# Ternary feed-forward of a perceiver kernel: both products of a tile in a row, its second activation first, the integers on POOL

## The reference

```python
def _layernorm(x, axis=-1, eps=1e-05):
    ...
def activation_quant(x, num_bits=8):
    ...
    s = qp / jnp.clip(jnp.max(jnp.abs(xf), axis=-1, keepdims=True), EPS, None)
    return (jnp.clip(jnp.round(xf * s), qn, qp) / s).astype(x.dtype)
def bit_linear(x, w):       # quantised x (8 bits) by ternary w
    ...
def rms_norm(x, weight, eps=RMS_EPS):
    ...
    return weight * (xf * jax.lax.rsqrt(var + eps)).astype(x.dtype)
h = jax.nn.silu(bit_linear(x, w_gate)) * bit_linear(x, w_up)   # 1024 rows x 1024
h = rms_norm(h, ln_weight)
return bit_linear(h, w_down)                                   # 1024 rows x 256
```

## Time and profile before

| what | us |
|---|---|
| median of 3 runs | 792.42 (791.86 to 793.72) |
| the profiled execution, its own time | 794.29 |
| its span, from the first to the last instruction | 792.1 |
| PE busy | 692.1 (87%) |
| DVE busy | 587.2 (74%) |
| ACT busy | 426.1 (54%) |
| POOL busy | 371.4 (47%) |
| the ternary layer in the span | from 208.82 (its first transposes) to 274.95 (end of its last `add`) |
| mean granted clock of TensorE, as a share of full speed | 0.943 |

### The profile page before, as it was taken

How to read it: one execution, slowest core, us unless ns; L and a number is a source line. 1 busy time by engine, 2 the same in 40 slices (tenths; PEclk the granted TensorE clock), 3 DMA queues, 4 the chain that set the end, 5 groups by cost and what they waited for, 6 DMA issues and landing times. The chain is left out here.

```text
span 792.1 us, 15843 instructions
## 1 busy us (share of the span) xinstructions
PE 692.1 (87%) x5487; PEld 466.5 (59%) x5490; DVE 587.2 (74%) x1156; ACT 426.1 (54%) x1314; POOL 371.4 (47%) x317
## 2 busy tenths in 40 slices
PE   5997899997666599999996899889999999999776
PEld 4664677786324354434334676567777776776644
DVE  4466799766788566656674889888888898788487
ACT  2565777653467312222335787156555645559664
POOL 1503555382246124334494555366676766666100
PEclk9999999999679579999996999999999999999989
DMA  6455000000300030720010000012211313320001
GB/s 197 122 172 226 1 2 1 2 1 1 93 2 1 0 113 19 235 69 26 1 40 1 2 2 1 21 42 61 61 52 48 110 62 97 83 90 3 1 3 52
DMA packets 33571, 41.91 MB, mean 53 GB/s; under 512 B 15072, under 2 KB 23264, under 8 KB 32608
## 3 DMA queue, kind: packets, MB, share of 16 engines
q1 hardware_dynamic: 33504, 41.06, 16.9%
HBM read 40.00 MB, written 1.05 MB: 52 GB/s over the span
## 5 line engine op out<-in xcount | busy, mean ns | idle before, releaser
L2094 POOL TENSOR_TENSOR ra_direct<-ra_direct,ra_crossed 128x512 f32<-128x512 f32 x64 | 81.2, 1268 | 80.2 <-DVE ra_crossed L2270 80.0
L717 ACT ACTIVATE c_probs<-bank,c_neg_max 128x128 f32<-128x128 f32 x256 | 91.2, 382 | 29.2 <-DVE c_neg_max L800 29.2
L2270 DVE SCALAR_TENSOR_TENSOR ra_crossed<-bank,ra_bias,ra_sin 64x512 f32<-64x512 f32 x128 | 95.9, 750 | 1.9
L753 POOL TENSOR_TENSOR c_probs<-c_probs,c_inverse 128x512 f32<-128x512 f32 x64 | 66.5, 1040 | 62.1 <-DVE c_inverse L771 62.1
L1557 POOL TENSOR_TENSOR r_turned<-r_times_a,r_times_b 128x1024 f32<-128x1024 f32 x24 | 56.4, 2351 | 72.3 <-DVE r_times_b L1756 72.3
L717 ACT ACTIVATION_READ_ACCUMULATOR c_probs<-bank,c_neg_max 128x1 f32 x256 | 56.6, 221 | 0.0
L2222 ACT ACTIVATE ra_probs_t<-bank 64x256 f32<-64x256 f32 x64 | 24.1, 377 | 58.4 <-PE bank L2164 58.0
L2228 ACT ACTIVATE ra_probs<-ra_masked,ra_neg_max 128x64 f32<-128x64 f32 x128 | 43.0, 337 | 18.2 <-DVE ra_neg_max L2290 17.9
L1837 POOL TENSOR_TENSOR ra_w_lo<-ra_raw,ra_w_hi 128x768 f16<-128x768 f32 x32 | 52.6, 1645 | 0.0
L58 PE MATMUL bank<-xt_hi,ra_w_hi 128*128 128x512 f16 x128 | 49.1, 383 | 0.9 <-PEq L599 0.9
L58 PE MATMUL bank<-xt_hi,ra_w_lo 128*128 128x512 f16 x128 | 49.0, 383 | 0.0
(11 more groups left out here) (280 smaller groups left out, 2093.7 us busy)
## 6 DMA issues: line engine op xcount, KB each, us to landing
ra_raw<-l_attn_w_dram SPq DMA_DIRECT2D x32, 384.0 KB, 3.0
wq<-l_wq_dram SPq DMA_DIRECT2D x16, 256.0 KB, 2.8
wo<-l_wo_dram SPq DMA_DIRECT2D x16, 256.0 KB, 3.4
wkcq<-l_wkcq_dram SPq DMA_DIRECT2D x16, 192.0 KB, 2.8
ra_wo<-l_attn_wo_dram SPq DMA_DIRECT2D x1, 2048.0 KB, 10.1
wqr<-l_wqr_dram SPq DMA_DIRECT2D x16, 96.0 KB, 2.9
wkv<-l_wkv_dram SPq DMA_DIRECT2D x16, 64.0 KB, 3.0
x_res<-x_dram SPq DMA_DIRECT2D x2, 512.0 KB, 7.5
```

Of the source, the lines that this page charges most:

```text
L717: e = nc.scalar.activation(probs[u][:, n, :], score_bank[u][q][:, n - q * HP, :], ACT.Exp, bias=neg_max[u][:, n:n + 1], accum_out=total[u] ...
L753: nc.gpsimd.tensor_tensor(out=probs[u][:, at, :], in0=probs[u][:, at, :], in1=inverse[u][:, at].unsqueeze(2).broadcast_to([P, HP, L]), op= ...
L2094: nc.gpsimd.tensor_tensor(out=direct[e][k][:], in0=direct[e][k][:], in1=crossed[k][:], op=ALU.add).then_inc(roped, 1)
L2270: ins = nc.vector.scalar_tensor_tensor(dst[out_lo:out_lo + rows].rearrange("p t (b s) -> p (t b) s", b=2), src[lo:lo + rows], bias[e][lo:l ...
```

## The change

The second `multiply` of a tile moves up on DVE, right behind the first. The second `silu` of a tile moves to the head of ACT's step. `integers` leaves DVE and goes to POOL, between the power of tile i-1 and the weighting of tile i. PE's list is the same.

```diff
--- before.py
+++ after.py
@@ -1298,14 +1298,30 @@
             nc.gpsimd.memset(magic[:], ROUND).then_inc(filled, 1)
             inputs.rstd(pool, PAIRS_X - 1)
             first.gpsimd(pool)
-            for t in range(TILES):
+            def integers(t):
+                pool.wait_ge(rounded, t + 1)
+                wait(pool, h_turned, t - 1)
+                nc.gpsimd.tensor_scalar(h_int[t % 2][:], hw[t % 2][:], ROUND, QUANT_MAX,
+                                        ALU.subtract, ALU.min).then_inc(h_ready, 1)
+
+            def weigh(t):
                 pool.wait_ge(multiplied, 2 * t + 2)
                 wait(pool, h_ready, t - 1)
                 nc.gpsimd.tensor_tensor(out=hw[t % 2][:], in0=h[t % 2][:], in1=m.ln_weight[:],
                                         op=ALU.mult).then_inc(weighted, 1)
+
+            def size(t):
                 pool.wait_ge(mean_done, t + 1)
                 nc.gpsimd.tensor_tensor(out=rms[:, t:t + 1], in0=mean_sq[:, t:t + 1], in1=m.minus_half[:],
                                         op=ALU.pow).then_inc(rms_done, 1)
+
+            for i in range(STEPS - 1):
+                if has(i - 1):
+                    size(i - 1)
+                if has(i - 2):
+                    integers(i - 2)
+                if has(i):
+                    weigh(i)
             for q in range(2):
                 ln.rstd(pool, q)
 
@@ -1395,12 +1411,12 @@
             keep_x(1)
             silu(0, 0)
             for i in range(STEPS):
+                if has(i):
+                    silu(i, 1)
                 if has(i - 1):
                     sum_squares(i - 1)
                 if has(i - 2):
                     round_h(i - 2)
-                if has(i):
-                    silu(i, 1)
                 if i in TURNS:
                     keep_x(TURNS[i])
                 if has(i + 1):
@@ -1443,12 +1459,6 @@
                 nc.vector.tensor_scalar(down_scale[:, at], h_max[:, at], m.ffn_mean[:, 2:3], 1.0 / QUANT_MAX,
                                         ALU.mult, ALU.mult)
 
-            def integers(t):
-                dve.wait_ge(rounded, t + 1)
-                wait(dve, h_turned, t - 1)
-                nc.vector.tensor_scalar(h_int[t % 2][:], hw[t % 2][:], ROUND, QUANT_MAX,
-                                        ALU.subtract, ALU.min).then_inc(h_ready, 1)
-
             def add(t):
                 dve.wait_ge(down_done, t + 1)
                 nc.vector.scalar_tensor_tensor(m.x[:, t, :], down_bank[t % 2], down_scale[:, t:t + 1],
@@ -1458,13 +1468,9 @@
             for i in range(STEPS):
                 if has(i):
                     multiply(i, 0)
+                    multiply(i, 1)
                 if has(i - 1):
                     sizes(i - 1)
-                if has(i - 2):
-                    integers(i - 2)
-                if has(i):
-                    multiply(i, 1)
-                if has(i - 1):
                     scales(i - 1)
                 if i == STEPS - 1:
                     ln.scale(dve, 0)
```

## The result

| kernel | median us | ratio to the kernel before | 95% interval |
|---|---|---|---|
| before | 792.14 (4 runs) | | |
| changed | 820.67 (4 runs, 819.05 to 821.31) | 1.0354 | 1.0332 to 1.0376 |

The change costs 28.5 us, where 6.9 were forecast. The profiled execution's span is 818.9 us, 26.8 more than before. The ternary layer, from its first transposes to the end of its last `add`, is 96.50 us long (207.74 to 304.24) where it was 66.13, so it lost 30.37 us.

The account below looks back on a forecast made before the run. DVE's own list was taken as the bound in steps with a fold, 5.47 us; afterwards a loop through the transposes. Terms +0.60, +5.73, -0.28 gave +6.05, clock +0.88: +6.9 us, 792.4 to 799.3, range 795.5 to 803.5.

Parts of the forecast that it names:

- Onto POOL: Integers moved to POOL: one instruction per tile was taken at 1.05 us, bounds 0.95 to 2.36 or 2.78 us.
- the integers are dear: Rival: POOL's integers take 2.36 us, giving 808.5 us, or 2.78, giving some 811; chance 10%.
- The loop: Third layer, transposes to next transposes through ACT, DVE and POOL: 6.81 us with a fold against 5.47, 5.95 without.
- to the first transposes: Piece 1, up to the layer's first transposes: second multiply ahead of mean square and power, +0.60 us.
- five loops: Piece 2, from the first transposes to tile 5's: 32.74 us against 27.01 before, +5.73.
- from tile 5's transposes to the end: Piece 3, to the last `add`: tile 6's integers +0.36, its `add` starting earlier -0.64, together -0.28 us.
- The power: POOL's power in each step: 0.55 us without DVE's integers beside it, where step 6 had 0.87.
- The clock: PE at its lower clock level after long waits: 0.88 us a loop, one of three loops counted, +0.88.
- What would show it: Profile signs: period 6.0 us without a fold, 6.8 with; near 8 means the integers' price was wrong.

Follow-up runs that it names:

- e1: Kernel of only one-input POOL instructions, nothing running beside them, against no kernel: subtract with min took 3.62 us, the pairs the program had used 1.04.
- e2: Changed kernel with POOL's integers made by add and multiply instead of subtract and min, limit at 127 left out: 798.54 us, 1.0075 of the kernel before.
- e9: Changed kernel with integers by add and multiply, that instruction run twice per tile, first into a spare tile: 807.35 us, 1.0220 of the kernel before.
- e3: Changed kernel with the integers back on DVE between sizes and scales, the rest of the change kept: 795.72 us, 1.0038 of the kernel before.
- e6: Kernel before with integers still on DVE but between first multiply and magnitude, and ACT rounding first: 788.88 us, 0.9963 of the kernel before.
- e10: Kernel before with only the integers moved to POOL, behind the power, made by add and multiply: 794.32 us, 1.0039 of the kernel before.
- e5: Kernel before with integers on POOL by add and multiply, ahead of the power, and ACT rounding first: 785.85 us, 0.9908 of the kernel before.

## Why the prediction was wrong

The time lies 17 us above the range, and one term did nearly all of it.

**The step that failed** is "Onto POOL": "1.05 us, which I take". The rows behind it were an interpolation over the number of columns, between rows whose pairs of operations were min with max and multiply with add. The slope of 0.82 ns a column was right and belongs to those pairs only. Subtract with min takes 3.63 us. The one row that warned, a single multiply of the same size at 2.78 us, was set aside because its rows have gaps; e1 shows 2.78 us without gaps. So the reason given was false, and 2.78 was no upper bound either. The rule of the Trainium skill (GPSIMD Engine Reference, Key points), a factor of about 2 against DVE, was nearer in direction but gave 1.37 us. Against DVE's 0.69 us for subtract with min in e1, POOL's dear pair is 5.2 times as long (3.62) and the cheap one 1.5 times (1.04; DVE wasn't timed with it).

**The rival "the integers are dear"** was the right one, at 10%. It was priced at seven places and at most 2.78 us. With 3.63 us and the 8.7 us per us between e2 and e9, neither of which uses the changed kernel's time, the forecast of 799.3 becomes 799.3 + 8.7 x 2.58 = 821.7, and 820.67 was measured.

**The loop** was right. The pieces of the layer, in us:

| piece | forecast | with 3.63 for 1.05 | measured in the change | measured in e2 |
|---|---|---|---|---|
| to the first transposes | +0.60 | +3.18 | 229.91 - 207.74 less 19.05: +3.12 | +0.41 |
| five loops | +5.73, clock +0.88 | +19.51 | 49.19 less 27.01: +22.18 | +6.64 |
| from tile 5's transposes to the end | -0.28 | +4.88 | 25.14 less 20.07: +5.07 | -0.10 |
| sum | +6.93 | +27.57 | +30.37 | +6.95 |

The five loops are 2.7 us above the third column, and 2.4 of it can be read. 1.29 is clock: the second loop too began at the low level (+0.41), and two of three loops with a fold did (+0.88 more than the one counted). The step from the power to the integers takes 0.65 and not 0.52 (+0.64 in all; in e2 it is 0.51). The two multiplies take 1.37 and not 1.20 in three loops (+0.51), since the second waits for its up product, which PE makes at the low clock: 1.06 us for the two matmuls at 261.02 in the change. So this is clock too, a term that the prediction had at nothing, and the clock's share is 1.80. In the loop of e2 that begins at the low clock the up product comes at full clock again, and DVE's two multiplies take 1.19 (250.36 to 251.55), as in its other two loops with a fold. In the last piece both tiles' integers count: at that price tile 7's own chain ends last and no longer the statistics, so there are eight places and not seven.

**The power** went from 0.87 to 0.56 us as forecast. That the shared ports are the cause, as the Trainium skill (SBUF — State Buffer, Who interferes with whom) has it, agrees with e3 (0.86 with DVE's `tensor_scalar` beside it) and e6 (0.54 with the same instruction elsewhere in the step).

**The clock** was the weakest estimate, one loop in three; it was right for e2's profiled execution and low for the change, where all three loops with a fold had up products at the low clock and two began there. That a long wait of PE brings it down is not a rule the traces bear out loop by loop: before the transposes at 248.28 PE stood idle 4.35 us and they ran at full clock, before those at 257.95 it was 4.08 and they did not.

**What would show it** named this case: a period near 8 us means that the price of the integers was wrong. It was 9.2 to 10.6. The other signs of the loop came too: DVE waits 5.33 us for `big_lo` and 0.44 between the scaling of the magnitude and `h_max` (forecast 0.3), and PE stands idle 4.1 to 5.3 us ahead of the transposes in the loops with a fold (forecast nearly 3, at 1.05 us for the integers).

## What to carry to other kernels

In these runs the price of a one-input instruction on POOL hangs on its pair of operations and not only on its size: before moving work there, find a row with the same pair in the same order, or run the pair alone once. Where a moved instruction is a link of a loop over several in-order engines, its full time is paid once a tile, and even a cheap one costs until it stands in its new engine's list where its input is already there; then the relieved engine's gain appears. With the cheap pair on POOL, the order (what ACT does first, and the integers ahead of the power) was worth 8.5 us (e10 to e5), the engine in that order 3.0 (e6 to e5).

## What the runs showed of the hardware that was not expected

On POOL, 128x1024 f32 with two operations against constants takes 1.04 us for add-multiply, multiply-add, multiply-multiply and min-max, and 3.62 to 3.65 us for the thirteen other pairs that ran, among them add-add, min-min, max-min and everything with subtract. A single operation takes 2.77 to 2.78 us, so a multiply by 1 behind an add (1.04 us) is cheaper than the add alone (2.77). bf16 or f32 out makes no difference. On DVE the dear pair takes 0.69 us (e1).
